# Queries, keys and maxima turned in 32x32 blocks by VectorE, with the token order and the values' path changed to fit

## The reference

```
x = x + 0.5 * moe(layernorm(x))
x = x + attention(layernorm(x))
x = x + 0.5 * moe(layernorm(x))

attention(x):                               # 16 heads of 16 dimensions
  q, k, v = x @ wq.T, x @ wk.T, x @ wv.T
  q, k = rope(rms(q)), rope(rms(k))
  y = softmax(q @ k.T / 4 + 1) @ v          # over all 1024 tokens of the batch
  return y @ wproj.T

moe(x):                                     # 8 experts, one per token, capacity 512
  route = argmax(x @ w_switch + b_switch); position = count of earlier tokens of that expert
  kept tokens: relu(x @ w1 + b1) @ w2 + b2; the others pass through
```

## Time and profile before

| | |
|---|---|
| time, median of 3 runs | 2152.18 us (2148.09 to 2154.19) |
| the profiled execution's own time | 2156.22 us |
| its span, first to last instruction | 2154.3 us |
| busy: PE, DVE, ACT, POOL | 2077.9, 1725.6, 1684.0, 987.9 us |
| attention, first to last reduction | 330.8 to 1854 us |
| granted PE clock over the span | 0.986 of full speed |

### The profile page before, as it was taken

One profiled execution on the slowest core, in us unless ns is written; L12 is line 12 of the kernel. 1 busy time (PEld: TensorE's weight loads), 2 busy tenths in 40 slices (PEclk: granted clock), 3 DMA queues, 4 the chain that ended last, 5 costly groups with the idle time before them and its releaser, 6 DMA issues.

```text
span 2154.3 us, 39634 instructions
## 1 busy us (share of the span) xinstructions
PE 2077.9 (96%) x14658; PEld 1073.5 (50%) x14658; DVE 1725.6 (80%) x2558; ACT 1684.0 (78%) x3255; POOL 987.9 (46%) x1221
## 2 busy tenths in 40 slices
PE   5799999999999999999999999999999999999997
PEld 4588975433444444444444444444444333236987
DVE  7776769988879888987988798888879889436774
ACT  5566647888888898988898898989888888755664
POOL 5786438652751672285067227614840201104542
PEclk9899999999999999999999999999999999899999
DMA  7454414345443444335433434435442425203331
GB/s 252 140 188 171 148 59 84 70 102 113 80 88 74 96 93 96 70 91 123 74 77 81 101 64 94 110 78 86 76 108 46 88 42 119 61 4 129 118 130 57
DMA packets 137857, 208.94 MB, mean 97 GB/s; under 512 B 30527, under 2 KB 95295, under 8 KB 137408
## 3 DMA queue, kind: packets, MB, share of 16 engines
q1 hardware_dynamic: 129792, 189.14, 36.9%
q0 software_dynamic: 7680, 16.87, 2.5%
q10 hardware_dynamic: 192, 0.39, 0.1%
HBM read 128.87 MB, written 72.01 MB: 93 GB/s over the span
## 4 chain that ended last, share of the span: by engine, by line
PE 71%; DVE 9%; issue 2%; DMA 1%; ACT 1%; SPq 1%; POOL 0%; another core or an unknown queue 0%; POOLq 0%; ACTq 0%; DVEq 0%
PE PS L1146 22%; PE PS L1129 17%; PE PS L1112 13%; PE PS L1019 6%; DVE NMX L2402 5%; PE PS L1083 3%; PE PS L826 2%; PE PS L981 1%; PE PS L983 1%; PE PS L982 1%; PE PS L961 1%; PE PS L963 1%; PE PS L962 1%; PE PS L1154 0%; DVE ST L1782 0%
## 5 line engine op out<-in xcount | busy, mean ns | idle before, releaser
L2402 DVE TENSOR_REDUCE NMX<-PS 128x1 f32<-128x1024 f32 x1024 | 1222.0, 1218 | 192.9 <-PE PS L1112 178.4
L1560 ACT ACTIVATE PB<-PS 128x512 f32<-128x512 f32 x2048 | 1104.0, 604 | 148.4 <-PE PS L1129 111.6
L1129 PE MATMUL PS<-QF,KF 51*128 51x512 f32 x2048 | 772.8, 457 | 5.5 <-ACT R L1523 2.2
L1112 PE MATMUL PS<-KF,QF 49*128 49x512 f32 x2048 | 726.4, 442 | 8.8 <-DVE NMX L2402 7.2
L1146 PE MATMUL PS<-PB,V 128*17 128x512 f32 (+1 forms) x5768 | 584.6, 477 | 0.0
L1129 PEld LDWEIGHTS PS<-QF,KF 51*128 51x128 f32 x2048 | 317.0, 185 | 419.1 <-ACT PB L1560 220.9
L1112 PEld LDWEIGHTS PS<-KF,QF 49*128 49x128 f32 x2048 | 310.5, 184 | 161.6 <-DVE NMX L2402 90.8
L1146 PEld LDWEIGHTS PS<-PB,V 128*17 128x17 f32 x5768 | 95.7, 95 | 235.6 <-issue 162.8
L2039 DVE TENSOR_TENSOR HLR<-HL,HHR 128x512 fp32r<-128x512 f32 x128 | 92.1, 720 | 87.2 <-ACT HHR L1476 79.5
L981 PE MATMUL PS<-W2H,HLR 128*128 128x256 f32 x512 | 143.0, 279 | 0.0
L983 PE MATMUL PS<-W2H,HHR 128*128 128x256 f32 x512 | 141.7, 277 | 0.0
(11 more groups left out here) (351 smaller groups left out, 3107.1 us busy)
## 6 DMA issues: line engine op xcount, KB each, us to landing
W<-in_w SPq DMA_DIRECT2D x32, 1024.0 KB
QF<-qs SPq DMA_DIRECT2D x186, 128.0 KB
KF<-qs SPq DMA_DIRECT2D x186, 128.0 KB
qs<-HI SPq DMA_DIRECT2D x64, 256.0 KB, 2.1
qs<-R1R SPq DMA_DIRECT2D x62, 256.0 KB, 2.3
QX<-x2d SPq DMA_DIRECT2D x8, 1024.0 KB, 5.4
out_x<-QX SPq DMA_DIRECT2D x8, 1024.0 KB, 5.0
YT<-YU SPq DMA_DIRECT2D x124, 64.0 KB, 3.9
```

Of the source, the lines that this page charges most:

```text
L1112: m = e.matmul(PS[:, 2 * i + half, :], QF[k][at:at + ROWS_S, p * SEQ + ti * 128:p * SEQ + ti * 128 + 128], KF[k][at:at + ROWS_S, p * SEQ + ...
L1129: e.matmul(PS[:, bank, :], KF[k][at:at + ROWS_ST, p * SEQ + sbk * 128:p * SEQ + sbk * 128 + 128], QF[k][at:at + ROWS_ST, p * SEQ + th * 51 ...
L1560: e.activation(PB[j % 3][:, h * 512:(h + 1) * 512], PS[:, place["e", tile], :], ACT.Exp).then_inc(e_out, 1)
L2402: e.tensor_reduce(NMX[:, u % 2, at:at + 1], PS[:, 2 * i:2 * i + 2, :], AX.XY, ALU.max, negate=True).then_inc(s_max, 1)
```

## The change

- **Queries and keys.** From batch 1 on, a DVE instruction (STREAM_TRANSPOSE, 128x512, line 2472 of the new kernel) turns QR directly in SBUF. It turns 32x32 blocks only: tokens 32i to 32i+31 of each 128 stay on partitions 32i to 32i+31, which now carry dimensions. ACT rounds that block once, from SBUF; its second copy goes. Four DMAs a piece put both parts into DRAM in runs of 128 numbers, 32 a batch where there were 16. The layout in DRAM is new, so that a unit comes back in eight DMAs, the high part broadcast to two sets of rows.
- **Token order.** Within each 512 tokens the order of keys and queries is now another one. YU is written back in the old order by the access pattern of the copy out of PSUM (`spread_back`). The values have to follow the keys: V17 is stored to DRAM and read back with its rows permuted in eight DMAs (`key_rows`), and the eight logit columns that POOL needs in the old order are read into a tile of their own (XR).
- **Maxima.** In all units DVE turns the 128x32 maxima itself, copies them rounded and subtracts; PE's transpose and ACT's two copies go. The rows travel in eight DMAs of 32-number runs instead of four of 128-number runs.
- **Tables.** Due steps of most side work are set anew, HALVED has 31 steps instead of 27, and at step 58 PE's side work stands in the middle of the step.

The place of the first example is PE's queue at steps 31 and 32 of the fifth batch, before; L826 turns a piece, L1083 is a tile of the output projection, L1093 turns the maxima.

The core of the diff:

```diff
-QK_AT = (16, 17, 19, 22, 23, 24, 30, 33)
+QK_AT = (16, 17, 18, 22, 25, 27, 30, 32)
-PIECES = ((29, 0, 0), (32, 0, 1), (37, 0, 2), (40, 1, 0), (42, 0, 3), (43, 1, 1), (44, 1, 2), (46, 1, 3))
+PIECES = ((29, 0, 0), (31, 0, 1), (36, 0, 2), (39, 1, 0), (42, 0, 3), (43, 1, 1), (46, 1, 3), (48, 1, 2))
...
+            def split(b):                                  # DVE
+                for k, at, hf, j, m in pieces(b):
+                    n = 8 * b + k
+                    yield at
+                    e.wait_ge(rope_out[hf], 4 * b + 8)
+                    e.wait_ge(st_q[n % 2], stored_in(n // 2))
...
+                    e.transpose(raw_of(n).rearrange("d (g t r) -> d g t r", g=4, t=4),
+                                QR[:, 4 * hf:4 * hf + 4, j * 128:(j + 1) * 128].rearrange("p t (g d) -> p g t d", g=4)
+                                ).then_inc(sp_full, 1)
...
             def maxima(u):                                 # DVE
-                yield UNIT + 1
-                e.wait_ge(mt_hi, u + 1)
+                yield MAX_AT[0]                            # 16
+                e.wait_ge(s_max, 32 * u + 32)
+                e.transpose(MR[:, p, :], NMX[:, p, :]).then_inc(mt_out, 1)
+                yield MAX_AT[1]                            # 16.5
+                e.wait_ge(mt_out, 3 * u + 1)
...
+                e.tensor_copy(MT[:, p, 0, :], MR[:, p, :]).then_inc(mt_out, 1)
+                yield MAX_AT[2]                            # 17
+                e.wait_ge(mt_out, 3 * u + 2)
                 e.tensor_tensor(MT[:, p, 1, :], MR[:, p, :], MT[:, p, 0, :].bitcast(F32), ALU.subtract
...
             def split(b, ...):                             # ACT
+                    if b == 0:
+                        e.copy(hi_of(n), PS[:, place["split", n], :])
+                        e.copy(raw_of(n), PS[:, place["split", n], :]).then_inc(sp_raw, 1)
+                    else:
+                        e.copy(hi_of(n), raw_of(n)).then_inc(sp_raw, 1)
...
+            def key_rows(b):                               # SP
+                yield values_at(b, 7) + 3
+                e.wait_ge(v_out, 8 * (b + 1))
...
+                e.dma_start(v_d.rearrange("(t p) f -> p t f", p=128), V17[b % 2]...[:, :, 0:ROW_V]).then_inc(st_v, 16)
+                yield values_at(b, 7) + 6
+                e.wait_ge(st_v, 16 * b)
+                for hf in range(2):
+                    for q in range(4):
...
+                        e.dma_start(V17[b % 2][32 * q:32 * q + 32, 4 * hf:4 * hf + 4, ...],
+                                    v_d[at:at + 128, :].rearrange("(i r) f -> r i f", r=32)).then_inc(ld_v, 16)
...
             def load_max(u):
...
+                    e.wait_ge(mt_out, 3 * u + 2 + pc)
+                    rows_q = QF[u % 3][ROWS_S + pc:128:64, :].bitcast(F32).rearrange("s (a i q) -> s a i q", i=4, q=32)
+                    for i in range(4):
+                        e.dma_start(rows_q[:, :, i, :], MT[32 * i:32 * i + 32, u % 2, pc, :].bitcast(F32)
```

More of the change, by code:

```diff
@@ L29 @@
 ROW, SENT = 524, 260
+ROW_V = 17 * H + NE
 WIDE = D + NE
@@ L1086, in post @@
                     busy[bank] = (pj_out, 8 * b + t + 1)
-            def maxima(u):
-                yield 16
-                e.wait_ge(s_max, 32 * u + 32)
-                bank = ring("mt", u)
-                take(bank)
-                e.transpose(PS[0:32, bank, 0:128], NMX[:, u % 2, :], IDN).then_inc(mt_full, 1)
-                busy[bank] = (mt_hi, u + 1)
             def score(n, i, half):
@@ L1334, in tensor_program @@
                     side.begin(n, split(0))
-                    prepare(side, BEGIN[1], 1, pre_x, split, values)
+                    prepare(side, BEGIN[1], 1, pre_x, None, values)
                 for k in range(2, NB):
                     if n == BEGIN[k]:
-                        prepare(side, n, k, pre_x, split, values)
+                        prepare(side, n, k, pre_x, None, values)
                 if r == 0 and 1 <= b < NB:
@@ L1343, in tensor_program @@
                     side.begin(n, leaving())
-                if n % UNIT == 0 and n < NS:
-                    side.begin(n, maxima(n // UNIT))
                 j = n - LAG
@@ L1355, in tensor_program @@
                     weigh(j - LATE, 0, 256 if halved else 512)
+                middle = n < NS and n % BATCH in MIDDLE
+                if middle:
+                    side.run(n)
                 for half in range(2):
@@ L1373, in tensor_program @@
                     again(AGAIN[0])
-                side.run(n)
+                if not middle:
+                    side.run(n)
             e.wait_ge(s_max, 32 * NU)
@@ L2464, in vector_program @@
                 if n == 0:
-                    prepare(side, BEGIN[1], 1, pre_x)
+                    prepare(side, BEGIN[1], 1, pre_x, split)
                 for k in range(2, NB):
                     if n == BEGIN[k]:
-                        prepare(side, n, k, pre_x)
+                        prepare(side, n, k, pre_x, split)
                 if r == 0 and 1 <= b < NB:
```

152 lines of the change are left out of this document (99 added, 53 removed).

## The result

| | before | after |
|---|---|---|
| median of 5 runs (lowest to highest) | 2152.14 us (2148.09 to 2154.19) | 2334.14 us (2329.51 to 2337.80) |
| ratio after to before, 95% interval | | 1.0845 (1.0828 to 1.0861) |
| profiled execution: span, mean granted clock | 2154.3 us, 0.986 | 2335.6 us, 0.937 |

I had forecast 2137 us in a range of 2113 to 2165, with 0.20 for slower. The kernel is 182 us slower: the forecast is wrong, and no rival of mine comes near.

A forecast was written before the change was run, and what follows sets the result against it. PE, busy 96% of the span, or its waits bound the kernel, nearly tied with DVE in plain steps. Gains 0.7 + 0.2 + 1.2 + 0.3 - 0.25 = 2.15 us a batch, 15 in seven, gave 2137 us, range 2113 to 2165.

The forecast's parts named there:

- What I cost at nothing, and its cover: ACT's savings, moved sums, changed DMA issues (SP about 13 us more in 194) and the values' round trip: no cost.
- 23 to 31: Stretch with four turned blocks and no projection: between -0.6 and +0.45 us a batch, taken as 0.2 gained.
- 32 to 39: Stretch with two turned blocks, one set of maxima, eight output-projection tiles: PE's 1.46 us come out nearly whole, 1.2 gained.
- plain steps are tied: Steps without side work: PE (2.31 to 2.44 us) and DVE (2.26 to 2.44) nearly tie, so added DVE work costs its time.
- The turned block: DVE's turning of 128x512 numbers: 0.6 us occupied by analogy with nearest trace rows; the skill's figures give 0.71.
- Rival C: Turned block on DVE at two cycles an element, 1.2 us: +1.45 us a batch, +10 us, median 2162; chance 0.14.
- counted as 0: New projections table moving one to three DVE sums into or out of plain steps: -0.6 to +0.6 us a batch, taken as 0.
- -0.25: Four more halved steps: half of 0.5 us a batch lost, as each costs 0.13 us where PE decides.
- A wait that is new: DVE waits for POOL's scaling and the store two pieces earlier; cover about 2 us at step 27, else once a batch.
- Rival D: Maxima rows in 32-number runs land late, delaying step 20's transposed score: 0.8 us a unit, 22 us, median 2159; chance 0.08.
- rivals A: DVE hides all added work in its 26 us idle: all 37 us come, median 2115, batch 188.6; chance 0.16.
- B: Blocks outside the projections cost the 0.6 us their split cost: 2 us gained in all, median 2150, batch 193.6; chance 0.18.

The follow-up runs named there:

- experiment 1: Changed kernel with the high parts' two copies loaded by separate 16-row transfers, twelve loads a unit instead of eight: 2130.12 us, ratio 0.9885 to the kernel before.
- experiment 7: Twelve-load version of the changed kernel with every table that sets side work as before the change: 2198.32 us, ratio 1.0167 to the kernel before.
- experiment 14: Twelve-load version of the changed kernel with only the old list of halved steps (27 instead of 31): 2138.68 us, ratio 0.9930 to the kernel before.
- experiments 11: Twelve-load version of the changed kernel with only the old tables for pieces and projections: 2183.03 us, ratio 1.0126 to the kernel before.
- experiment 15: Twelve-load version of the changed kernel with only the old steps for the projections of queries and keys: 2150.68 us, ratio 0.9985 to the kernel before.
- 16: Twelve-load version of the changed kernel with only the old routing tables (LATER, SOONER): 2161.76 us, ratio 1.0051 to the kernel before.
- experiment 10: Changed kernel, eight loads kept, with the four RC<-YU transfers of a unit issued from ScalarE's queue instead of SyncE's: 2245.71 us, ratio 1.0433 to the kernel before.
- experiments 3: Changed kernel with only the queries' high parts in the 2 x 16 form, the keys' by 16-row transfers, ten loads: 2156.66 us, ratio 1.0014 to the kernel before.
- 13: Changed kernel, ten loads, only the queries' second high part and low part paired in a 2 x 16 transfer, nothing read twice: 2143.22 us, ratio 0.9947.
- experiment 4: Changed kernel without the XR load of 32-byte runs, POOL taking those numbers from the turned values: 2327.13 us, ratio 1.0804 to the kernel before.
- experiment 2: Kernel before with only its high-part loads changed to the 2 x 16 form that reads the source twice, still twelve loads: 2277.66 us, ratio 1.0565.

## Why the prediction was wrong, step by step

**"What I cost at nothing, and its cover": the failed step.** The edit that lost 204 us stood in it with a count: "loads 32 of 0.5 for 48", together with "SP gets about 13 us more of issue in 194". I priced issues and bytes, and never asked on how many DMA engines a transfer runs. The bytes were equal, the issues fewer, so I took it for free. What stood in its place before is in the earlier trace rows and in the stretch from 1160 to 1170 us above: twelve loads at a DMA share of 0.92, and RC landing 5.7 us after its issue, well inside the time until RECIPROCAL (some 14 us in the changed kernel). What the runs showed instead of nothing: four loads a unit on two engines for 20 us, 27 waits of 4.4 us for RC on VectorE, and 204 us with what they bring on PE; with the loads as twelve, none of it. The diff had the form `[n, 16, 2048]`, and by the rule of the Trainium skill's page cited above it stood there to be read; I weighed another section of that page.

**The clock.** No step of mine counted it. Of the 201.4 us between the spans of the changed kernel and of experiment 1, PE's waits for NMX are 130.4 - 14.4 = 116 us, PE's busy time for the same work, at the lower clock, 2129.1 - 2055.8 = 73 us, and PE's waits for KF 11.1 - 1.6 = 9.5 us.

**The rest of the change, by experiment 1.** I forecast a batch of 191.7 us; it has 190.6, and before 193.7. So a full batch gains 3.1 us where I forecast 2.15. That the total of 15 us nearly comes out is luck: in the profiled executions the eight batches of experiment 1 differ from those of before by +5.3, -4.1, -3.3, -2.8, -3.1, -3.3, -3.1 and -2.0 us, 16.4 less in all. Batch 0 is longer, which no term of mine has; its cause is open. The last is shorter, for which I counted nothing. The ratio 0.9885 makes 24.8 us; of what is over, some 4 us lie outside attention in the two profiled executions, and why isn't shown. By stretches, experiment 1 minus before in the step table:

| steps | forecast | measured |
|---|---|---|
| 16 to 22 | -0.7 | +0.04 |
| 23 to 31 | -0.2 | -0.40 |
| 32 to 39 | -1.2 | -2.56 |
| 0 and 48, maxima | -0.3 | -0.24 |
| the other steps | +0.25 spread over the batch | +0.1 |

That plain steps are tied fits where the tables did not move anything: with the old tables (experiment 7) steps 16 to 22 are 0.52 us shorter than before where I forecast 0.7, and 23 to 31 0.03 longer where I forecast 0.2 shorter. My sign of being wrong there, a stretch 23 to 31 that grows, came with the changed kernel (24.45 to 33.70 us), but from the waits for RC; in experiment 1 the same stretch has 24.46. Steps 32 to 39 gave twice the forecast, 1.74 of it at step 32. There PE had a turned piece, an output projection and the maxima's transpose; the new table puts that piece at step 36, and the projection alone stays. I costed the move nowhere. A small misreading: the 0.28 us of a maxima transpose is its busy time; at 1198.63 in the trace of before it occupies 0.20.

**The turned block.** I took 0.6 us occupied; the prediction's other estimate, from the Trainium skill, "VectorE: DVE Perf Modes", section "The three transpose paths", was 0.71. It is busy 0.695 us (mean of 56, experiment 1) and occupies 0.64: 1279.76 to 1280.40 in the changed kernel. Rival C, two cycles an element, is out.

**The tables: "counted as 0" and "-0.25".** The sign of the halved steps was wrong: the new list, four steps longer and with others moved, gives 1.15 us a batch, and going back to the old one costs 0.45% (experiment 14). The others are no matter of tenths either, but for the values: put back singly they cost 4.1 (projections of queries and keys), 5.3 (routing) and 0.5 us a batch (values), the projections and pieces together 7.8, all tables 11.1. I costed them as sums that move on VectorE. What pieces, projections and routing do besides, by experiments 11, 15 and 16, is keep the waits for a stored piece, for GpSimd and for the maxima rows out of the path.

**"A wait that is new".** I named VectorE's wait for the store two pieces earlier and for GpSimd, and gave it 2 us of cover at step 27. The wait for the store is real, but at steps 31 and 32: 3.2 us in all in experiment 1, 30.8 in 11. The wait for GpSimd at step 27 does not come in the changed kernel or in experiment 1. It comes in experiment 15, 0.9 to 1.2 us a batch, when the last projection stands a step later as before: the place was named rightly, and the new table of projections is its cover.

**Rival D** is wrong for the changed kernel and right for its neighbours: with SyncE held, the eight issues of maxima rows are what PE waits for (experiments 7 and 16). For rivals A and B: experiment 1's batch of 190.6 us lies between A's 188.6 and B's 193.6, nearest to the forecast's 191.7.

## What to carry to other kernels

Before a transfer's form is changed, write down its outermost dimension on both sides and the number of DMA engines that follows. A transfer that reads its source twice by an outer dimension of 2 saves issues and takes seven eighths of the engines away; the rate falls from 125 to 52 GB/s here. In the trace it shows as a DMA share near 0.12 while what was issued behind it on the same queue lands some 20 us late. And count what stands behind an in-order wait: 4.3 us of late rows, once a unit, cost 7 us each time by PE's wait and the clock after it (204 us in 28).

The version to keep is experiment 1, the changed kernel with twelve loads: 1.15% (0.90 to 1.41%) faster than before.

## What the runs showed of the hardware

- Four transfers of 4 KB issued behind loads on two engines: 56 of 64 semaphore increments within 4.3 us of the first issue, the last eight after 19.4 to 20.4 us; from ScalarE's queue (experiment 10) the last eight come after 4.7 to 8.7 us.
- A DMA issue does not always take its 0.6 us: with the unit loads on two engines and XR's 1024 runs of 32 bytes behind them an issue of RC on the same queue took up to 16.3 us, with half of such loads (experiments 3 and 13) up to 10.4 and 9.3; without XR (experiment 4) at most 1.50, with twelve loads (experiment 1) at most 1.54; in the kernel before with such loads (experiment 2), which has no XR, at most 5.2.
- A transfer on two engines moves 52 GB/s, 8192 bytes in 0.312 us on each. The stretch of a unit load with twelve transfers moves 125 GB/s in experiment 1 and 135 in the kernel before, so 2.4 to 2.6 times as much and not eight times: in experiment 1 a packet of 8192 bytes takes 0.99 us there (median from 1156 to 1166 us), over three times its time on the two.
- After an idle of 7.76 us PE's granted clock is at 1.2 GHz for 5.3 us more; a score matmul takes 0.79 us and not 0.50.
- A block of 128x512 numbers of 32 bits, turned in 32x32 blocks by VectorE, is busy 0.70 us and occupies 0.64, a 128x32 one of maxima is busy 0.20.
